# One more buffer for a raw operand, and the hand-written step order of all five engines set anew, in a blocked linear and LoRA kernel

## The reference, cut to what matters

```python
x = L0_attn_data
xn = _layernorm(x, axis=-1)
bm = mask.reshape(Nb, BH, Kb, BW).sum(axis=(1, 3)) > 0          # 32 x 32 blocks
wb = weight.reshape(Nb, BH, Kb, BW) * bm[:, None, :, None]
s = jnp.einsum('bsk,nk->bsn', xn, wb.reshape(N, K)) + bias
q = jnp.einsum('bi,ki->bk', xn.mean(axis=1), Wq)
coeffs = softmax(jnp.einsum('bk,ek->be', q, lora_keys) / math.sqrt(K))
base = jnp.einsum('bsi,oi->bso', xn, W_org)
h = jnp.einsum('bsi,eir->bser', xn, lora_down)
delta = jnp.einsum('be,bser,ero->bso', coeffs, h, lora_up)
out = x + s * silu(base + delta)
```

## Time and profile before

| | us |
|---|---|
| median of 3 runs | 440.56 (438.39 to 443.45) |
| the profiled execution, whole | 440.17 |
| its span in the trace | 438.5 |
| PE busy | 424.7 |
| DVE busy | 334.7 |
| ACT busy | 216.4 |
| POOL busy | 104.9 |
| DMA moved | 101.05 MB, 230 GB/s over the span |

### The profile page before, as it was taken

One profiled execution on the slowest core, in us unless ns is written; L12 is line 12 of the kernel. 1 busy time (PEld: TensorE's weight loads), 2 busy tenths in 40 slices (PEclk: granted clock), 3 DMA queues, 4 the chain that ended last, 5 costly groups with the idle time before them and its releaser, 6 DMA issues.

```text
span 438.5 us, 5903 instructions
## 1 busy us (share of the span) xinstructions
PE 424.7 (97%) x1910; PEld 345.7 (79%) x1910; DVE 334.7 (76%) x492; ACT 216.4 (49%) x379; POOL 104.9 (24%) x91
## 2 busy tenths in 40 slices
...
GB/s 299 413 416 240 161 266 255 280 210 218 195 237 264 265 290 283 290 325 362 179 73 144 49 114 275 287 236 336 410 386 165 96 76 21 72 270 242 265 160 96
DMA packets 40862, 101.05 MB, mean 230 GB/s; under 512 B 4608, under 2 KB 4864, under 8 KB 40064
## 3 DMA queue, kind: packets, MB, share of 16 engines
...
...
HBM read 71.31 MB, written 29.36 MB: 230 GB/s over the span
## 4 chain that ended last, share of the span: by engine, by line
PE 75%; DMA 14%; DVE 4%; POOL 2%; SPq 2%; issue 1%; ACT 1%; DVEq 0%; ACTq 0%; POOLq 0%
PE psA L864 24%; PE psA L866 24%; PE psA L865 24%; DMA x_nat_sb<-in_x_nat_dram 4%; DMA d_dram<-d_split 3%; DMA a_raw<-in_up_dram 2%; DMA out_dram<-cst 2%; DMA worg_sb<-in_w_org_dram 2%; DMA b_hi<-d_dram 2%; PE psA L883 1%; DVE nat_stats L1154 1%; DMA temp<-in_down_dram 1%; SPq L796 1%; DVE cst L1323 1%; POOL x_nat_sb L1365 1%
## 5 line engine op out<-in xcount | busy, mean ns | idle before, releaser
L864 PE MATMUL psA<-b_hi,a_hi 128*128 128x512 f32 (+1 forms) x444 | 173.6, 391 | 0.5 <-ACT snaps L1107 0.5
L866 PE MATMUL psA<-b_hi,a_lo 128*128 128x512 f32 (+1 forms) x444 | 172.1, 388 | 0.0
L865 PE MATMUL psA<-b_lo,a_hi 128*128 128x512 f32 (+1 forms) x444 | 172.0, 387 | 0.0
L864 PEld LDWEIGHTS psA<-b_hi,a_hi 128*128 128x128 f32 x444 | 83.4, 188 | 18.4 <-ACT snaps L1107 0.9
L866 PEld LDWEIGHTS psA<-b_hi,a_lo 128*128 128x128 f32 x444 | 83.4, 188 | 17.1
L865 PEld LDWEIGHTS psA<-b_lo,a_hi 128*128 128x128 f32 x444 | 83.4, 188 | 16.6
L1078 ACT ACTIVATE b_hi<-b_raw 128x512 fp32r<-128x512 f32 (+2 forms) x66 | 45.3, 716 | 56.0 <-DVE b_raw L1232 36.5
L1219 DVE TENSOR_TENSOR b_lo<-b_raw,b_hi 128x512 fp32r<-128x512 f32 (+2 forms) x66 | 52.0, 814 | 8.6 <-ACT b_hi L1078 8.3
L1395 POOL TENSOR_TENSOR cst<-cst,xres 128x512 f32<-128x512 f32 x15 | 23.0, 1534 | 98.7 <-DVE cst L1323 98.7
L1107 ACT ACTIVATE snaps<-psA 128x512 f32<-128x512 f32 x39 | 23.2, 595 | 42.8 <-PE psA L866 42.6
L1219 DVE TENSOR_TENSOR a_lo<-s_raw,a_hi 128x512 fp32r<-128x512 f32 x52 | 37.4, 733 | 5.2 <-ACT a_hi L1068 5.2
...
## 6 DMA issues: line engine op xcount, KB each, us to landing
...
```

Of the source, the lines that this page charges most:

```text
L864: nc.tensor.matmul(ps, l_hi, r_hi, start=first, stop=False, skip_group_check=True)
L865: nc.tensor.matmul(ps, l_hi, r_lo, start=False, stop=False, skip_group_check=True)
L866: return nc.tensor.matmul(ps, l_lo, r_hi, start=False, stop=over, skip_group_check=True)
```

## The change

A second semaphore and a second raw buffer for lora_down: chunk k goes to `temp[:, 2 + k % 2]`, and its load waits for `VD(k-2)` instead of `VD(k-1)` (the first two for the same step as before). `d_split` stays one buffer, and `Dk` still waits for `DS(k-1)`.

The order of all five engines' steps is new. PE has the same steps in nearly the same order (some `BP` one product earlier or later, `G0` before P51). SP has the same 280 steps. Among ACT, DVE and POOL some steps change the engine: POOL loses 9 in sum (26 out, 17 in), DVE gains 6 (22 out, 28 in), ACT gains 3. For example `LN1` and `LN2` go from POOL to DVE, `LN5` the other way, `W0.3` and `W1.1` from DVE to POOL; POOL adds x to 9 blocks instead of 15.

The code, whole, and of the order those lines that the prediction speaks of:

```diff
@@ ORDER, SP
-    LX0 LM0 LW0.0 LW0.1 LX1 LM1 LY LK LM2 LW1.0 LX2 LW1.1 LX3 LW2.0 LM3 LI LW3.0 LX4 RS0 LX5 RS1 RS2 ST2 RS3 LT7
+    LX0 LM0 LX1 LY LW0.0 LW0.1 LK LM1 LM2 LX2 LW1.0 LX3 LW1.1 LM3 LX4 RS0 LI LX5 LW2.0 ST2 RS1 LW3.0 RS2 RS3 LX6
...
-    ST32 ST35 DS0 DL1 RS13 ST37 RS12 ST38 DL2 DS1 ST39 LT15 LT14 DS2 DL3 ST42 LG8.1 LG8.0 RS15 ST44 DL4 DS3 RS14
-    ST45 ST46 DL5 DS4 LG9.1 LG9.0 ST49 DS5 DL6 LU0.0 ST51 LU0.1 ST52 DS6 DL7 LU0.2 LG10.0 LU0.3 DS7 ST55 LD0.4
-    LD0.6 LD0.5 LD0.7 LU0.7 LD0.0 LU0.4 LU0.6 LD0.1 LD0.2 LD0.3 ST58 LU0.5 ST56 ST57 LE0.0.0 LE0.0.1 LE0.1.0
+    LE0.1.2 ST32 ST35 ST37 DL2 RS13 DS1 LT15 LT14 ST38 DL3 ST39 RS12 DS2 ST42 ST44 DL4 LG8.1 DS3 LG8.0 RS15 ST45
+    DS4 DL5 ST46 RS14 DL6 LG9.1 DL7 DS5 ST49 ST51 LU0.0 LU0.1 LU0.2 DS6 LU0.3 LG9.0 DS7 ST52 ST55 LD0.4 LD0.6
+    LD0.5 LU0.7 LG10.0 LD0.7 LU0.4 LU0.6 LD0.0 LU0.5 LD0.1 LE0.0.0 ST58 LD0.2 LE0.0.1 LE0.1.0 ST56 ST57 LB0 LD0.3
...
-    LD1.4 LB14 LB13 LU1.3 LD1.6 ST77 LR13 ST79 LR14 LD1.1 LD1.0 LB15 LR15 ST80 LD1.3 LD1.7 LD1.2 LB18 LB17 LE1.1.2
-    ST84 LE1.2.2 ST85 LG14.0 LB19 LB16 LE1.3.2 ST86 LE1.0.2 ST83 LE1.0.1 LE1.1.0 LE1.1.1 LE1.0.0 LE1.2.1 LE1.2.0
+    LD1.6 LU1.3 LR13 LB14 ST77 LR14 ST79 LB13 LD1.1 LB15 LD1.0 LD1.3 LD1.7 ST80 LB18 ST84 LR15 ST85 LE1.1.2 LD1.2
+    LE1.2.2 LB17 ST86 LE1.3.2 LE1.0.2 LE1.0.1 LB19 ST83 LE1.1.0 LE1.1.1 LE1.0.0 LE1.2.1 LE1.2.0 LE1.3.0 LG14.0
@@ ORDER, ACT
-    PB6.1 H37 H36 QS40 H39 D2 H33 H35 QS42 H40 QS43 QO44 D3 H38 H44 H42 D4 H41 QS47 H45 H43 QS49 H46 D5 H47 QS50
+    H37 PB6.0 QS40 H36 H39 H33 D2 H35 QS42 QS43 PB7.1 QO44 D3 PB7.0 H40 D4 H45 H38 QS47 H42 H46 H41 H44 QS49 H43
...
+    D5 QO51 QS50 H47 D6 GE0 H48 QS53 U0.0 D7 U0.1 QS55 U0.2 U0.3 U0.7 QO57 U0.4 HB1.1.0 GE1 U0.6 HB1.1.2 U0.5
@@ ORDER, DVE
-    SN0 CA0.1 CB0 CM0 W0.0 W0.2 W0.1 VB0.0.0 VB0.0.2 VB0.0.1 W0.3 V4 SN1 CB1 R0 KD CM1 SN2 R1 SN3 W1.1 V0 V2 CA3.1
+    SN0 CA0.0 CB0 CM0 W0.1 W0.0 SN1 W0.2 R0 VB0.0.2 LN1 CB1 CM1 VB0.0.0 V4 SN2 KD R1 LN2 SN3 V5 V0 V2 VB0.1.0
...
-    QM79 QM77 VU1.1 QC80 QR79 VU1.2 QM80 V74 QC83 VU1.3 QC84 VU1.4 V75 QM85 QM84 VU1.5 VU1.7 QC86 QR85 V76 QM86
-    QM83 QR86 EA1.1.2 VU1.6 EA1.2.2 VB2.1.1 VB2.1.2 EA1.3.2 EA1.0.2 VB2.1.3 EA1.0.1 VB2.1.0 EA1.0.0 EA1.1.0 T2.0.1
+    QC80 S12.2 QM80 QR80 VU1.2 QC83 V74 V75 S12.4 VU1.0 VU1.5 VU1.1 QC84 QM85 VU1.3 QM84 VU1.4 VU1.6 QR85 V76 QC86
+    QM83 QR83 QM86 QR86 VU1.7 EA1.1.2 EA1.2.2 EA1.3.2 EA1.0.2 VB2.1.2 EA1.0.1 VB2.1.1 EA1.0.0 T2.0.1 VB2.0.0
@@ ORDER, POOL
-    SR0 LN0 SR1 LN1 W1.0 SR2 LN2 SR3 LN3 W2.0 SR5 SR4 LN4 XR6 XR8 T0.0.2 XR7 XR9 XR10 S3.1 S3.3 XR11 XR12 XR13
+    SR0 LN0 W0.3 SR1 W1.0 SR2 W1.1 SR3 LN3 W2.0 SR5 SR4 LN4 XR6 LN5 XR8 T0.0.2 XR7 XR10 XR9 S3.1 XR11 S3.3 XR12
@@ the code
-        d_loaded = sem("d_loaded")
+        d_loaded = [sem(f"d_loaded{i}") for i in range(2)]
...
-            return d_split[:, 1, :], temp[:, 3, :], d_split[:, 0, :]
+            return d_split[:, 1, :], temp[:, 2 + st[1] % 2, :], d_split[:, 0, :]
...
-                    if k == 0:
+                    if k < 2:
                         wait_lo(sp, ("B", 0, T1, 0))
                     else:
-                        wait_lo(sp, ("D", k - 1))
-                    sp.dma_start(temp[:, 3, :], down_t[k]).then_inc(d_loaded, 16)
+                        wait_lo(sp, ("D", k - 2))
+                    sp.dma_start(temp[:, 2 + k % 2, :], down_t[k]).then_inc(d_loaded[k % 2], 16)
...
-                    act.wait_ge(d_loaded, 16 * (k + 1))
+                    act.wait_ge(d_loaded[k % 2], 16 * (k // 2 + 1))
...
-                    nc.scalar.activation(d_split[:, 0, :], temp[:, 3, :], ACT.Copy).then_inc(act_hi, 1)
+                    nc.scalar.activation(d_split[:, 0, :], temp[:, 2 + k % 2, :], ACT.Copy).then_inc(act_hi, 1)
```

More of the change, by code:

```diff
@@ new lines @@
+    LE0.1.1 LB2 LB1 LB3 LE0.2.0 LE0.2.1 LE0.3.0 LE0.3.1 LE0.0.3 LE0.1.3 LU1.4 LE0.2.3 LE0.3.3 LR1 LR0 LR3 LG10.1
+    LG11.0 LU1.5 ST64 LU1.6 LR2 LU1.7 LG11.1 LB6 LB5 LR5 LB4 ST65 LR6 LR4 ST60 LB9 LB7 ST70 LB10 ST72 LG12.0 LR9
+    ST67 LR10 ST66 LR8 LB8 LR7 LG12.1 LR12 LG13.0 ST74 LB12 LU1.0 LU1.1 LB11 LG13.1 ST73 LR11 LU1.2 LD1.5 LD1.4
+    LD1.6 LU1.3 LR13 LB14 ST77 LR14 ST79 LB13 LD1.1 LB15 LD1.0 LD1.3 LD1.7 ST80 LB18 ST84 LR15 ST85 LE1.1.2 LD1.2
+    LE1.2.2 LB17 ST86 LE1.3.2 LE1.0.2 LE1.0.1 LB19 ST83 LE1.1.0 LE1.1.1 LE1.0.0 LE1.2.1 LE1.2.0 LE1.3.0 LG14.0
@@ L115 @@
+    LE1.3.1 LB16 LE1.0.3 LE1.1.3 LE1.2.3 LE1.3.3 LR17 LR16 LG14.1 LR18 LR19 ST94 ST92 LR23 LB23 ST88 LG15.0 LR21
+    LB21 LB20 LR20 LG15.1 LR22 LB22 ST93 ST95 LB24 ST98 LR24 LB25 LR25 LB28 LB26 LB27 ST102 LR28 ST100 LR26 ST101
+    LB29 LR27 LB30 LR29 LR30 ST105 LB31 ST107 ST108 ST111 LR31 ST112 ST113 TS0 TS1
     """,
@@ L117 @@
     CP0 TX0.0 TX0.1 P0 K CP1 TX1.0 TX1.1 P1 TX2.0 TX2.1 P2 TX3.0 P3 TX3.1 CP2 P4 P5 CP3 P6 TX4.0 TX4.1 P7 P8 P9
-    P10 TX5.0 P11 P12 TX5.1 P13 P14 BP6 P15 P16 P17 BP7 BP8 P18 P19 P20 BP9 P21 P22 P23 P24 P25 P26 BP10 P27 P28
-    P29 BP11 BP12 P30 P31 BP13 P32 P33 P34 P35 BP14 BP15 P36 P37 P38 P39 P40 P41 P42 P43 P44 P45 P46 P47 P48 P49
-    P50 P51 G0 P52 P53 P54 P55 G1 P56 P57 P58 E0.0.2 E0.1.2 E0.2.2 E0.3.2 E0.0.0 E0.0.1 E0.1.0 E0.1.1 E0.2.0
+    P10 TX5.0 P11 P12 TX5.1 P13 P14 BP6 P15 P16 P17 BP7 P18 BP8 P19 P20 P21 BP9 P22 P23 P24 BP10 P25 P26 P27 P28
+    BP11 P29 BP12 BP13 P30 P31 P32 P33 P34 P35 P36 P37 P38 BP14 P39 BP15 P40 P41 P42 P43 P44 P45 P46 P47 P48 P49
+    P50 G0 P51 P52 P53 P54 P55 G1 P56 P57 P58 E0.0.2 E0.1.2 E0.2.2 E0.3.2 E0.0.0 E0.0.1 E0.1.0 E0.1.1 E0.2.0
     E0.2.1 E0.3.0 E0.3.1 E0.0.3 E0.1.3 E0.2.3 E0.3.3 P59 P60 P61 P62 P63 P64 P65 P66 P67 P68 P69 P70 P71 P72 P73
@@ L171 @@
[L171 to L173 removed]
+    CA0.1 TC0.0 H4 HB0.0.0 TC0.1 HB0.0.3 HB0.0.2 CA1.0 CA1.1 H6 TC1.0 HB0.0.1 CA2.1 TC1.1 H7 H5 HB0.1.0 CA2.0 H0
+    H2 HB0.1.1 TC2.0 CA3.0 H1 TC2.1 CA3.1 TC3.0 H3 TC3.1 HB0.7.0 H8 HB0.2.0 X6 TC4.0 H9 H10 BA6 X8 TC4.1 TC5.0 H11
```

83 lines of the change are left out of this document (37 added, 46 removed).

## The result

The changed kernel takes 443.44 us (median of 20 runs, 440.65 to 446.98), the kernel before, timed beside it, 439.17 us (20 runs, 438.23 to 443.76): a ratio of 1.0081, 95% interval 1.0057 to 1.0104. It is slower by 3.6 us by that ratio (4.3 us by the medians), where I had forecast 4.7 us faster. By the bound of 1% this is no change; it is clear of the noise all the same, it lies outside my range of 432.5 to 440.5, and it has the other sign. The runs scatter alike, with a standard deviation of 1.7 us after and 1.6 us before.

A forecast was written before the change was run, and what follows sets the result against it. PE, busy in 97% of the span, was taken to bound the kernel, so only its waits could change. From the profiled 440.17 us, 440.17 - 1.5 - 1.0 - 1.8 = 435.9 us, range 432.5 to 440.5.

The forecast's parts named there:

- What bounds the kernel: Whole kernel: PE is busy in 97% of the span, so the change can only win or lose PE's waits.
- Term A: Start of the kernel: earlier LN1 and LN2 shorten PE's waits, -1.5 us, bounds 0 to -3.6.
- The mask's and `LN1`'s part: Start: second mask there by 15.6, LN1 no longer the limit, TX1.0 near 18.2, PE gains 0.9 us.
- `LN2` on DVE 0.80: Start: LN2 takes 0.80 us on DVE and ends at 23.9, so TX2.0 starts at 24.0 instead of 25.28.
- Term B: lora_down path: PE's two stalls, at P49 and E0.1.2, shrink, -1.0 us, bounds -1.8 to +0.5.
- P49's half: lora_down path: less ahead of store DS3, D4 starts near 159, and P49's snapshot stall of 0.7 us goes.
- The second half: lora_down path: E0.1.2's stall waiting for LD0.5 goes from 1.1 us to about 0.8.
- Term C: Second batch's matrix: LE1.0.2 lands earlier and PE's stall for it goes, -1.8 us, bounds -1.8 to +1.
- 2.6 us less in the queue: Second batch's matrix: LE1.0.2 goes ahead of LG14.0, LB19 and LB16, landing at 326.2.
- Moves costed at nothing: Steps changing engine and other moves: covered between waits on PE, cost 0; without any cover 4 us would be PE's.
- stall C: PE's wait for LE1.0.2 before E1.1.0; rival: ST80 lands late, it grows to 2.8 us; 0.11 shared with another late step.
- another step comes late by several us: Anywhere in the order: a moved step is late, kernel no faster; chance 0.11 together with stall C growing, 0.07 above 445.

The follow-up runs named there:

- `two_buffers`: Kernel before with only the second raw buffer of lora_down, all engines' step order as before: ratio 1.002 to the kernel before.
- `c_alone`: Kernel before, one raw buffer, with QR83 on DVE behind QM83 and LG14.0, LB19, LB16 behind LE1.0.2 and ST83 on SP: ratio 0.9958.
- `all_three`: Changed kernel with W1.1, LN5 back on DVE, DS5, DS6 earlier; behind 235 us old order plus the edits of `c_alone`: ratio 0.9908 to the kernel before.
- Experiment 4: Two buffers, old order before 235 us; behind it only SP's order new: 1.0187, or only the other engines' new: 1.0028, to the kernel before.
- experiment 3: Changed kernel, one repair each: QS83 ahead of U1.2 on ACT 1.0060; on SP, LG13.0 and LG13.1 later 1.0069, or four moves undone 1.0055.

## Why the prediction was wrong, by its own steps

**What bounds the kernel.** Right: every us lost or won in the pair of traces was a wait of PE, or the clock behind one.

**Term A (-1.5 us, came 0).** The mask's and `LN1`'s part was right: `TX1.0` at 18.45 (18.2 forecast), and the granted clock stayed at 1.00, where it had been 0.50. The step that failed is "`LN2` on DVE 0.80". I took the 0.80 us from a row beside which POOL had only a step of one column (`SR4`, 128x1), and had left out that the change puts `W1.1` beside `LN2`. `TX2.0` came at 26.04 and not at 24.0. The row that should have told me, a DVE multiply of 1.78 us beside POOL, I used only for waits that the change takes away. The Trainium skill (SBUF — State Buffer, Who interferes with whom) lists `tensor_scalar` among the operations that can ask for the pair of ports shared with POOL, and says that the loser waits for the whole instruction; here the trace agrees in the main, 2.53 us with `W1.1` beside it and 0.82 without, 1.7 us more where `W1.1` takes 1.91. The move of `LN5` to POOL I had not priced at all; it made PE wait 1.0 to 1.8 us in three of eight executions and not at all in the others.

**Term B (-1.0 us, came 0).** P49's half came true: `D4` started at 159.47 (159 forecast) and the stall went. The count behind it was short, since `LG8.0` (512 KB) went behind `DS3` as well as `RS15`; that `DS3` gained 1.2 us, close to the 1.3 forecast, is in part luck. The second half, "1.1 us of stall become about 0.8", failed: the wait was 1.5 us. PE came 0.5 us earlier, and `LD0.5` took 7.05 us where it had taken 6.86. In 17 profiled executions this load took 5.2 to 7.3 us, and PE's wait for it went from none to 2.4 us with it; a few tenths of forecast there are below what the chip repeats. The orders overlap, but not evenly: with the old order before 235 us it took 5.2 to 5.7 us in four of seven, with the new one 6.2 to 7.1 in all ten. Whether the new order makes this load slower is not tested. That the second buffer is worth nothing by itself agrees with `two_buffers`.

**Term C (-1.8 us, came -1.1).** The mechanism was right, as `c_alone` shows with its full 1.8 us. The mis-sized term is the "2.6 us less in the queue". Less the 3.9 us by which PE was late, `LE1.0.2` was issued at 322.2 (322 forecast) and landed at 327.7 (326.2 forecast): it took 5.5 us, where the sum had 4.2. I had counted what `LE1.0.2` passes and not `LD1.2` (512 KB), which the new order puts behind `LE1.1.2`, ahead of `LE1.0.2`. That this made the difference is not shown: in `c_alone` `LD1.2` stands where it stood, and `LE1.0.2` took 5.45 us all the same (4.65 in `all_three`). There the stall went because `LE1.0.2` was issued 1.3 us earlier against PE.

**Moves costed at nothing (came +4.0 us).** This is the step that turned the sign. I had gone through the moves near the stalls that I knew and through the low parts, with SP's queue only where one of the three terms needed it. `LG12.0`, `LB8`, `LR12`, `LG13.0` and `LG13.1` change places ahead of P85, where there was no stall before. `QS83`, two steps behind `U1.2` before and three now, had 1.7 us to spare then (done at 304.33, P85 at 306.01), and `U1.2` came 3.1 us later. So the term that stood at nothing measured +4.0 us. Experiment 4 shows that the wait before P85 comes with SP's new line, and experiment 3 that neither of the two repairs tried on it is enough by itself; which set of its moves is the least that makes the loss is open. The snapshot's place on ACT decides only which tile pays.

**The rivals.** The change did come out slower, but not by the mechanism that I had priced for that side: `ST80` took 6.3 us and not 14, and stall C shrank. The case that did come, "another step comes late by several us", had a share of 0.11, of it 0.04 below 445 where the result lies, and was outside the range. For an order in which most of SP's line was moved that share was too small, and the range allowed a new wait of 1 to 3 us at its upper end, where the one that came was 4.0.
